# Making the context's bf16 parts for a masked attention earlier, inside the projection of a latent attention

## The reference

```python
q = lat @ Wq
kv_input = jnp.concatenate([x, lat], axis=1)
k, v = jnp.split(kv_input @ Wkv, 2, axis=-1)
```

```python
scores = jnp.einsum('bhqd,bhkd->bhqk', qh, kh) + encoder_attention_mask
weights = jax.nn.softmax(scores, axis=-1)
ctx = jnp.einsum('bhqk,bhkd->bhqd', weights, vh)
return jax.nn.relu(ctx @ wo_w.T + wo_b)
```

## Time and profile before

| | |
|---|---|
| time, median of 3 runs | 4953.37 us |
| the profiled execution: span | 4944.8 us |
| busy: PE, DVE, ACT, POOL | 4178.6, 2876.8, 2358.9, 1360.7 us |
| granted TensorE clock over the span | 0.897 |
| latent projection (96 plain units) | 2579 to 2749 us |
| masked split stage (24 given units) | 4214 to 4290 us |

### The profile page before, as it was taken

One profiled execution on the slowest core, in us unless ns is written; L12 is line 12 of the kernel. 1 busy time (PEld: TensorE's weight loads), 2 busy tenths in 40 slices (PEclk: granted clock), 3 DMA queues, 4 the chain that ended last, 5 costly groups with the idle time before them and its releaser, 6 DMA issues. The chain is left out here.

```text
span 4944.8 us, 69703 instructions
## 1 busy us (share of the span) xinstructions
PE 4178.6 (85%) x20384; PEld 1982.2 (40%) x20384; DVE 2876.8 (58%) x6517; ACT 2358.9 (48%) x4572; POOL 1360.7 (28%) x1202
## 2 busy tenths in 40 slices
PE   8679866689689997897979799999997988189986
PEld 6322455386552333573334233333335644022224
DVE  4558474302668883106850477878863265398866
ACT  4347331243244774333743354545551255269993
POOL 0122141211111111112210387878880222000112
PEclk9669988799887998897989899999998999589998
DMA  8445212354043332663424322111201044623421
GB/s 283 114 105 122 53 38 34 145 194 149 19 142 57 70 61 92 248 219 116 95 83 153 107 66 65 66 61 61 75 29 38 32 121 87 206 52 92 95 55 37
DMA packets 330008, 486.55 MB, mean 98 GB/s; under 512 B 84404, under 2 KB 232484, under 8 KB 315092
## 3 DMA queue, kind: packets, MB, share of 16 engines
q1 hardware_dynamic: 322976, 449.92, 31.6%
q0 software_dynamic: 6384, 32.61, 2.1%
q10 hardware_dynamic: 348, 0.44, 0.0%
HBM read 327.63 MB, written 143.92 MB: 95 GB/s over the span
## 5 line engine op out<-in xcount | busy, mean ns | idle before, releaser
L1348 POOL TENSOR_TENSOR lc_totals<-lc_totals,lc_weights 128x1024 f32<-128x1024 f32 (+1 forms) x320 | 623.3, 1948 | 165.5 <-DVE lc_totals L1297 134.7
L1257 ACT ACTIVATE lc_weights<-ps 128x1024 f32<-128x1024 f32 x384 | 393.9, 1026 | 445.3 <-PE ps L1174 432.4
L1278 DVE TENSOR_REDUCE lc_part_max<-ps 128x2 f32<-128x1024 f32 x384 | 466.4, 1215 | 204.8 <-PE ps L1154 203.1
L1174 PE MATMUL ps<-lc_q,lc_k 64*128 64x512 f32 x1536 | 397.1, 595 | 4.3 <-issue 4.3
L1184 PE MATMUL ps<-lc_weights,lc_v 128*64 128x512 f32 x1536 | 371.7, 605 | 0.0
L858 DVE TENSOR_REDUCE l1x_core_part_max<-ps 128x1 f32<-128x512 f32 x512 | 316.5, 683 | 54.3 <-PE ps L682 54.2
L854 DVE CUSTOM_DVE_ANT_0 l3x_core_unused<-ps,l3x_core_mask_q 128x512 f32<-128x512 f32 x512 | 330.5, 686 | 6.0 <-DVE l3x_core_row_max L862 4.9
L817 ACT ACTIVATE l3x_core_weights<-ps 128x512 f32<-128x512 f32 x512 | 325.9, 689 | 8.0 <-PE ps L750 7.7
L817 ACT ACTIVATE l1x_core_weights<-ps 128x512 f32<-128x512 f32 x512 | 266.6, 605 | 83.4 <-PE ps L750 83.3
L800 ACT ACTIVATE ps<-l3x_core_mask_k 128x512 f32<-128x512 f32 x384 | 269.1, 701 | 32.9 <-DMA l3x_core_mask_k<-in_mask_k 32.9
L682 PE MATMUL ps<-l3x_core_k,l3x_core_q 96*128 96x512 bf16 x512 | 213.5, 418 | 53.2 <-DVE l3x_core_part_max L854 38.3
(11 more groups left out here) (493 smaller groups left out, 8589.7 us busy)
## 6 DMA issues: line engine op xcount, KB each, us to landing
cf_w<-in_L1f_w SPq DMA_DIRECT2D x32, 1024.0 KB, 7.2
lc_k<-latent_k SPq DMA_DIRECT2D x32, 768.0 KB, 6.5
lc_v<-latent_values SPq DMA_DIRECT2D x32, 768.0 KB, 5.0
latent_k<-feed_staged SPq DMA_DIRECT2D x64, 256.0 KB
latent_values<-feed_staged SPq DMA_DIRECT2D x64, 256.0 KB
k_heads<-proj_parts SPq DMA_DIRECT2D x40, 384.0 KB, 2.6
q_heads<-proj_parts SPq DMA_DIRECT2D x32, 384.0 KB, 2.6
q_heads<-proj_parts SPq DMA_DIRECT2D x32, 256.0 KB, 3.0
```

The source lines that it names most:

```text
L1174: mm = nc.tensor.matmul(out[j], k_tile[g % RING][strip(j), i * P:(i + 1) * P], q_tile[g % RING][strip(j), :], start=False, stop=True)
L1257: nc.scalar.activation(weights[:, i % TILES, :, :], k.ps[:, B0 + (i % 2) * HEADS:B0 + (i % 2 + 1) * HEADS, 0:nq], ACT.Exp, scale=scale).th ...
L1278: nc.vector.reduce_max(own, k.ps[:, A0:A0 + HEADS, :], AX).then_inc(a_taken, 1)
L1348: nc.gpsimd.tensor_tensor(total, total, own, ALU.add).then_inc(added_by_pool, 1)
```

## The change

In the masked stage the 16 context units are gone, with the load of the context: only the 8 token units are left, with the two loads of weights among them. The latent projection gets the 16 context units, one behind every sixth plain unit, the last one at the end of the list. The context comes in 8 pieces of 512 KB (`la_ctxT`), each for two units; a piece is loaded when SP comes to the first of the two units before. PE's banks and semaphore counts go by `turn_of`, the number of a unit among those that PE makes, since given units now lie between them.

```diff
--- before.py
+++ after.py
@@ -108,6 +108,7 @@
     nc = k.nc
     splits = [n for n, u in enumerate(units) if u[0] in ("split", "given")]
     made = [n for n, u in enumerate(units) if u[0] != "given"]
+    turn_of = {n: i for i, n in enumerate(made)}
     staged = any(u[0] in ("value", "plain") for u in units)
     VALUES = 6
     stored_by = []
...
@@ -180,11 +181,11 @@
                 unit = units[n]
                 if n in late_of:
                     pe.wait_ge(late_in[late_of[n]], 16 * len(late[late_of[n]][1]))
-                if n >= 8:
-                    pe.wait_ge(evacuated, n - 7)
+                if turn_of[n] >= 8:
+                    pe.wait_ge(evacuated, turn_of[n] - 7)
                 rows = P if unit[0] == "split" else unit[2]
                 for cols, lhsT, rhs, start, stop in unit[1]:
-                    last = nc.tensor.matmul(k.ps[0:rows, n % 8, cols], lhsT, rhs, start=start, stop=stop)
+                    last = nc.tensor.matmul(k.ps[0:rows, turn_of[n] % 8, cols], lhsT, rhs, start=start, stop=stop)
                 last.then_inc(ready, 1)
 
         @block.scalar
...
@@ -200,7 +201,7 @@
             i = j = 0
             for n, unit in enumerate(units):
                 if unit[0] != "given":
-                    act.wait_ge(ready, n + 1)
+                    act.wait_ge(ready, turn_of[n] + 1)
                 if unit[0] == "given":
                     if n in late_of:
                         act.wait_ge(late_in[late_of[n]], 16 * len(late[late_of[n]][1]))
...
@@ -328,6 +329,13 @@
     return [("split", [(slice(0, width), weight[:, c, m * P:(m + 1) * P], source(c, t), c == 0, c == CH - 1) for c in range(CH)],
              width, None if bias is None else bias[:, m:m + 1], store.rows(m, t, width))
             for t in range(B * store.n // width) for m in range(CH)]
+
+
+def given_units(source, store):
+
+
+    return [("given", source[:, m, t * BANK:(t + 1) * BANK], BANK, None, pick(store, slice(m * P, (m + 1) * P), slice(t * BANK, (t + 1) * BANK)))
+            for t in range(store[0].shape[2] // BANK) for m in range(CH)]
 
 
 def value_units(source, rows, weight, store):
...
@@ -2849,14 +2857,8 @@
     with nc.sbuf_tensor("l3x_att", [P, NG, T], F32) as att, \
             nc.sbuf_tensor("l3x_ow", [P, CH, C], F32) as ow, nc.sbuf_tensor("l3x_ob", [P, C], F32) as ob:
         q_parts, k_parts = k.q_parts, k.k_parts
-        with nc.sbuf_tensor("l3x_ctxT", [P, CH, TC], F32) as ctxT:
-            def as_is(src, store):
-                return [("given", src[:, m, t * BANK:(t + 1) * BANK], BANK, None, pick(store, slice(m * P, (m + 1) * P), slice(t * BANK, (t + 1) * BANK)))
-                        for t in range(store[0].shape[2] // BANK) for m in range(CH)]
-
-            project_stage(k, as_is(k.xT, q_parts) + as_is(ctxT, k_parts), [],
-                          late=[(T // BANK * CH, [(ctxT[:], inp["ctxT"])], 0)],
-                          prefetch=[(ow[:], inp["L3x_out_w"]), (ob[:], inp["L3x_out_b"].partition_broadcast(P))])
+        project_stage(k, given_units(k.xT, q_parts), [],
+                      prefetch=[(ow[:], inp["L3x_out_w"]), (ob[:], inp["L3x_out_b"].partition_broadcast(P))])
         dense_att = k.xT
         attention_stage(k, "l3x_core", ChannelParts(q_parts), ChannelParts(k_parts), inp["ctx"], S, SC, 1.0, att, mask=(inp["mask_q"], inp["mask_k"]), dense_att=dense_att, finish=False,
                         raw_values=True)
@@ -2889,7 +2891,13 @@
                 own = slice(b * S + i * P, b * S + (i + 1) * P)
                 units += [("plain", [(slice(0, BANK), latT[:, c, own], w[:, c, 2 * INNER + v * BANK:2 * INNER + (v + 1) * BANK], c == 0, c == CH - 1)
                                      for c in range(CH)], P, values[(b * NK + SC) // P + i, :, v * BANK:(v + 1) * BANK]) for v in range(INNER // BANK)]
-        project_stage(k, units, [])
+        with nc.sbuf_tensor("la_ctxT", [P, CH, TC], F32) as ctxT:
+            given = given_units(ctxT, k.k_parts)
+            units = spread_among(units, given, 0)
+            at = [units.index(given[CH * t]) for t in range(TC // BANK)]
+            pieces = [slice(t * BANK, (t + 1) * BANK) for t in range(TC // BANK)]
+            project_stage(k, units, [], late=[(n, [(ctxT[:, :, own], inp["ctxT"][:, :, own])], at[t - 1] if t else 0)
+                                              for t, (n, own) in enumerate(zip(at, pieces))])
     with nc.sbuf_tensor("la_att", [P, ICH - CH, T], F32) as att:
         def att_of(g):
 
```

More of the change, by code:

```diff
@@ L159, in _ @@
                 elif unit[0] != "kept":
-                    sync.wait_ge(evacuated, n + 1)
+                    sync.wait_ge(evacuated, turn_of[n] + 1)
                     sync.dma_start(unit[3], value[0:unit[2], j % VALUES].rearrange("p h d -> p (h d)")
@@ L211, in _ @@
                 elif unit[0] == "kept":
-                    nc.scalar.activation(unit[3], k.ps[:, n % 8, 0:C], ACT.Copy).then_inc(evacuated, 1)
+                    nc.scalar.activation(unit[3], k.ps[:, turn_of[n] % 8, 0:C], ACT.Copy).then_inc(evacuated, 1)
                 elif unit[0] == "split":
@@ L221, in _ @@
                     for cols, column in bias if isinstance(bias, list) else [(slice(0, width), 0.0 if bias is None else bias)]:
-                        ins = nc.scalar.activation(full[:, i % 2, cols], k.ps[:, n % 8, cols], ACT.Identity, bias=column)
+                        ins = nc.scalar.activation(full[:, i % 2, cols], k.ps[:, turn_of[n] % 8, cols], ACT.Identity, bias=column)
                     ins.then_inc(evacuated, 1)
@@ L229, in _ @@
                     d = HD if unit[0] == "value" else QUAD
-                    nc.scalar.activation(value[0:rows, j % VALUES, :, 0:d], k.ps[0:rows, n % 8, 0:H * d].rearrange("p (h d) -> p h d", h=H),
+                    nc.scalar.activation(value[0:rows, j % VALUES, :, 0:d], k.ps[0:rows, turn_of[n] % 8, 0:H * d].rearrange("p (h d) -> p h d", h=H),
                                          ACT.Copy).then_inc(evacuated, 1)
@@ L257, in _ @@
                     whole = full[:, i % 2, 0:width]
-                    dve.wait_ge(evacuated, n + 1)
+                    dve.wait_ge(evacuated, turn_of[n] + 1)
                     if i >= 3:
```

## The result

The changed kernel took 4908.29 us (median of 4 runs, 4906.35 to 4910.83), the kernel before 4951.99 beside it: ratio 0.9915, 95% interval 0.9903 to 0.9928. That is 36 to 48 us less; the forecast was 40 less. A second comparison of the same two kernels gave 0.9924 (0.9910 to 0.9937), 31 to 44 us less. By the medians it is 43.7 us less in the first and 35.6 in the second, since the kernel before had 4951.99 in the one and 4944.11 in the other; the forecast lies between the two.

The account below looks back on a forecast made before the run. PE was taken to bound the latent projection, and the round trip of three buffers the masked stage. The terms −48.0 + 0 + 7.9 = −40.1 us took the median from 4953.4 to 4913 us, range 4902 to 4930.

Parts of the forecast that it names:

- What bounds the masked stage: Masked stage: no engine bounds it; it runs at the round trip of its three buffers, all 76 us on the path.
- The masked stage, −48.0: Masked stage: without 16 context units and their load, the core's first load comes 48.0 us sooner (39.8 to 52.0).
- the load's delay: Masked stage: the 4096 KB context load holds back the first token unit's store; removing it takes 8.7 us off.
- The body, 0 us: Latent projection: each round with a context unit takes 9.4 us, inside PE's 10.3, so added work costs 0 us.
- The end, +7.9: End of the projection's list: stores left after the last high part delay the core's first load 7.9 us (4.0 to 15.2).
- PE's clock and the masked core: After the masked stage: the core moves with the stage's end; PE's clock, at 0.50 until 4370, brings no gain or loss.
- From the span to the time: Whole kernel: the median stands 8.6 us above the profiled span, so a span of 4904.7 becomes 4913 us.
- a round longer than PE's on average: Rival, projection: rounds of 11.0 us cost 10 more (4923), of 12.0 cost 24 more (4937); chance 0.18.
- Slow first stores: Rival, masked stage: token units' first stores are slow by themselves, not for the load; 31.9 less, 4921; chance 0.05.
- Cheaper ends: Rival: 4.0 at the projection's end, up to 52.0 at the masked stage; 44 to 48 less, 4905 to 4909; chance 0.13.
- values land one after another: Rival, projection: held-back values land 2.0 us each, sixth at t + 16.9; round 17.5 us, 61 slower, 5014; chance 0.03.
- a fixed time paid six times: Projection bursts: an opposing rule; some 2 us per transfer paid serially makes a burst 18.5 us, losing about 150 us.

Follow-up runs that it names:

- the load kept: Changed kernel, but the masked stage still loads the whole 4096 KB context, which nothing reads: 4919.96 us, 0.9952 of the kernel before.
- six buffers: Changed kernel with low parts made at once, context units among the first 90 plain units, and six part buffers in the masked stage: 4893.28 us, 0.9903 of before.
- low parts at once: Changed kernel, but DVE makes a context unit's low part at once when a plain unit follows: 4902.54 us, 0.9910 of the kernel before.
- projection alone: Changed kernel, but the masked stage makes the context's parts too, as before, so they are made twice: 4957.37 us, 1.0029 of the kernel before.
- stored twice: Changed kernel, but each context unit's parts are first stored to a spare place in the projection: 4918.02 us, 0.9944 of the kernel before.

## Why the prediction was right

Step by step, by the working ahead:

- *What bounds the masked stage* (the round trip of three buffers): shown by the load kept, which puts 9 us back with nothing computed from it, and by six buffers, which take 5.8 us out.
- *The masked stage, −48.0*: −47.9 in the first trace, −47.2 in the second. Its terms too: the fourth unit 6.58 us behind the first (worked out: 6.6), the load's delay 8.6 to 9.4 (8.7), and from the last high part to the core's load 4251.87 − 4242.59 = 9.3 us (10.0). The total met the forecast so closely by luck: the last high part came 18.6 us behind the first where 17.9 were worked out, 0.7 more, and the end took 0.7 less.
- *The body, 0 us*: the high parts are 10.30 us apart. The round was worked out as 9.4; the shortest in the two traces of the changed kernel are 9.56 and the longest 11.62, and long ones were made up in the rounds behind them. PE's 384 matmuls took no longer for them, so its eight banks took up the lag. The term was right with less to spare than I had. I took one rate for all rounds. Stretches of a burst, of the list's end and of a long round (the one from 2609.47), with the columns of the earlier trace rows:

```profile
2675.00:2677.00 2.00, 2.00 (x6) 0.82 (x5) 0.00 (x0) 0.00 (x0) 0.00 (x0) 1.00 1.02 366
2748.00:2750.00 2.00, 0.00 (x0) 0.00 (x0) 0.00 (x0) 0.00 (x0) 0.00 (x0) 0.50 1.03 383
2617.00:2619.00 2.00, 2.00 (x6) 0.88 (x5) 0.00 (x0) 0.94 (x3) 0.00 (x0) 1.00 1.09 192
```

  In a burst the DMA engines are fully busy at 366 to 383 GB/s, near the 372 that I had taken, so its bytes bound it. In the long round they are fully busy too, for 2 us at half that rate. Why was not tried.
- *The end, +7.9*: the stage is 7.2 to 7.5 us longer, and T + 10.7 stands where T + 10.6 was worked out. The end by itself, from the last copy to the load, is 8.0 us longer (11.19 against 3.22); from PE's first matmul to the last copy it is 0.7 shorter (166.69 against 167.35), and kernels with the same work for PE also differ so there (167.3 with low parts at once).
- *PE's clock and the masked core*: the granted clock stood at 0.50 until 4336 in the trace after, 84 us behind the masked stage's end, and until 4370 before, 80 us behind it; no gain. The core moved with its stage.
- *From the span to the time*: this step was wrong in its reading, though it did no harm. I added 8.6 us to the span of the profiled execution. In the run that was profiled after, time and span are 4910.83 and 4909.0, so 1.8 us lie around a span. The rest, some 7 us, was a fast execution of the kernel before against slower timed ones: its median was 4951.99 in the first comparison and 4944.1 in the next two. 4944.8 − 40.1 + 1.8 gives 4906.5, nearer to the 4908.3 than my 4913. The span itself was 4909.0 where I had 4904.7: it has 5.0 us more between the two stages and 2.6 more behind the masked core's first load, and 2.8 less ahead of the projection. The second trace of the same kernel has only 0.9 of the 5.0, so at least 4 of them are drift. The place behind the masked core's first load is 2.4 us longer in that trace too, but also 1.8 longer in "projection alone", whose masked stage is that of before, so it isn't shown to come from the change.

Of the rivals, a round longer than PE's on average came only where I made it longer (stored twice). Slow first stores are out by the load kept. Cheaper ends, 4.0 us at the projection and up to 52.0 at the masked stage, did not come either: they were 7.3 and 47.9, though the median of 4908.29 alone would also fit them. That values land one after another is out by the six stores of one round, behind which ACT made five copies, each into the next buffer, within 3.4 us (2677.23 to 2680.57). The sixth copy, at 2681.08, waited for PE, so by then all six had landed, at most 9.6 us behind the high part and not 16.9. That a store lands some 3 us behind its issue in a burst, against 2.0 before, fits the full DMA engines of a burst; it is not a fixed time paid six times.

## What to carry to other kernels

Work whose inputs are ready early can be free in a stage that another engine bounds, as here in the body, but read the order and not only the sums: here a low part that was made one unit late held SP for a full round and left a margin under 1 us, which nothing in the busy shares showed. Put such work so that it ends before the host stage's own last unit; all that the change gave up, 7.3 us, lay there. And where no engine of a stage is busy half of the time and the DMA engines aren't full either, look at what its producer waits for: here it was stores of three units back, and six buffers took 5.8 of 28 us.

## What the runs showed of the hardware

A store of 256 KB landed 2.0 us (median) after issue where stores were issued at PE's pace, 1.72 us apart; in bursts of seven stores its median was 3.0 (`latent_k`, `latent_values`) to 3.5 us (`latent_q`); the DMA engines' share rose to 0.57 without slowing PE: 384 matmul records took 166.65 us, against 167.27. In such a burst the DMA engines moved 366 to 383 GB/s at a share of 1.0 (two stretches of 2 us in the trace after). A load of 4096 KB ahead of a store on the same issuing engine held that store back so that its waiter stood 11.9 to 12.2 us, in the three traces read for it (before, projection alone, load kept), against 3.5 without it.
